# AdaLN block with rank-1-scaled attention and an MLP: new on-chip addresses for the TensorE operands, and the two products of one weight tile issued in pairs

## The reference

```python
mod = (_silu(L0_c) @ L0_wmod).reshape(8, 6, 1, -1)
sa, ca, ga, sb, cb, gb = (mod[:, i] for i in range(6))
ga = (2 * (ga >= 0) - 1) * jnp.maximum(jnp.abs(ga), 0.25)      # the same for gb
h = _layernorm(x) * (1 + ca) + sa
scores = jnp.einsum('nsd,ntd->nst', h * w_lhs, h * w_rhs)
x = x + ga * jnp.einsum('nst,ntd->nsd', softmax(scores, axis=2), h)
h = _layernorm(x) * (1 + cb) + sb
x = x + gb * (relu(h @ W1 + b1) @ W2 + b2)
```

## Time and profile before

| | us |
|---|---|
| median of 3 runs | 682.03 (681.68 to 682.57) |
| the profiled execution, whole | 681.68 |
| its span in the trace | 679.9 |
| TensorE matmul busy | 675.1 (99% of the span) |
| TensorE weight load busy | 624.6 (92%) |
| VectorE busy | 546.8 (80%) |
| ScalarE busy | 500.2 (74%) |
| GpSimd busy | 295.6 (43%) |

### The profile page before, as it was taken

How to read it: one execution, slowest core, us unless ns; L and a number is a source line. 1 busy time by engine, 2 the same in 40 slices (tenths; PEclk the granted TensorE clock), 3 DMA queues, 4 the chain that set the end, 5 groups by cost and what they waited for, 6 DMA issues and landing times.

```text
span 679.9 us, 13532 instructions
## 1 busy us (share of the span) xinstructions
PE 675.1 (99%) x4551; PEld 624.6 (92%) x4551; DVE 546.8 (80%) x1139; ACT 500.2 (74%) x749; POOL 295.6 (43%) x311
## 2 busy tenths in 40 slices
PE   9999999999999999999999999999999999999998
PEld 8688899998999999998999989999899999999997
DVE  4798889887998879988799887988799887778321
ACT  2377787976789777895888958888678976747562
POOL 3551365225353345442545235542535333615543
PEclk9999999999999999999999999999999999999999
DMA  8131664237632478025671266423662246212210
GB/s 295 56 79 66 196 181 148 72 108 235 193 86 87 121 225 246 38 86 160 192 204 62 93 195 200 129 62 126 217 199 75 83 138 208 89 35 71 85 40 31
DMA packets 72897, 88.57 MB, mean 130 GB/s; under 512 B 6880, under 2 KB 64800, under 8 KB 72864
## 3 DMA queue, kind: packets, MB, share of 16 engines
q1 hardware_dynamic: 72864, 88.15, 42.1%
HBM read 51.66 MB, written 36.47 MB: 130 GB/s over the span
## 4 chain that ended last, share of the span: by engine, by line
PE 99%; DVE 0%; DMA 0%; issue 0%; SPq 0%
PE col L666 9%; PE col L667 9%; PE col L668 9%; PE acc L588 8%; PE acc L589 8%; PE acc L594 8%; PE score L773 8%; PE score L768 8%; PE score L770 8%; PE score L656 4%; PE score L657 4%; PE score L655 4%; PE score L761 4%; PE score L629 2%; PE score L557 1%; PE score L733 1%
## 5 line engine op out<-in xcount | busy, mean ns | idle before, releaser
L1256 POOL TENSOR_TENSOR hid_lo<-hid,hid_hi 128x512 fp32r<-128x512 f32 x127 | 176.2, 1390 | 259.8 <-ACT hid_hi L798 259.3
L794 ACT ACTIVATE hid<-col,b1T 128x512 f32<-128x512 f32 x128 | 87.2, 682 | 73.9 <-PE col L668 72.0
L588 PE MATMUL acc<-W2hi,hid_hi 128*128 128x256 f32 x480 | 119.3, 282 | 0.0
L589 PE MATMUL acc<-W2lo,hid_hi 128*128 128x256 f32 x480 | 117.9, 279 | 0.0
L666 PE MATMUL col<-h2hi,W1hi 128*128 128x512 f32 x256 | 100.3, 392 | 0.0
L667 PE MATMUL col<-h2lo,W1hi 128*128 128x512 f32 x256 | 100.2, 391 | 0.0
L668 PE MATMUL col<-h2hi,W1lo 128*128 128x512 f32 x256 | 99.7, 389 | 0.0
L798 ACT ACTIVATE hid_hi<-hid 128x512 fp32r<-128x512 f32 x128 | 81.0, 633 | 23.9 <-PE acc L594 16.3
L588 PEld LDWEIGHTS acc<-W2hi,hid_hi 128*128 128x128 f32 x480 | 90.6, 189 | 1.4
L589 PEld LDWEIGHTS acc<-W2lo,hid_hi 128*128 128x128 f32 x480 | 90.6, 189 | 1.3
L594 PE MATMUL acc<-W2hi,hid_lo 128*128 128x256 f32 x480 | 77.7, 279 | 0.0
(11 more groups left out here) (168 smaller groups left out, 1476.9 us busy)
## 6 DMA issues: line engine op xcount, KB each, us to landing
block_rows<-blocks SPq DMA_DIRECT2D x29, 512.0 KB, 2.8
blocks<-block_rows SPq DMA_DIRECT2D x116, 128.0 KB, 2.9
x_cur<-x SPq DMA_DIRECT2D x16, 512.0 KB, 3.9
ln_t<-x SPq DMA_DIRECT2D x14, 512.0 KB, 5.2
score_blocks<-stages SPq DMA_DIRECT2D x14, 512.0 KB, 3.1
S<-score_blocks SPq DMA_DIRECT2D x56, 128.0 KB, 2.9
S<-quarter_blocks SPq DMA_DIRECT2D x56, 96.0 KB, 2.5
out<-x_mlp SPq DMA_DIRECT2D x8, 512.0 KB, 5.1
```

The lines of the kernel that those rows point to most:

```text
L588: nc.tensor.matmul(o, hi, W2hi[:, it, :], start=(it == 0 and (apart or t % 2 == 0)), stop=False, skip_group_check=True)
L589: nc.tensor.matmul(o, hi, W2lo[:, it, :], start=False, stop=False, skip_group_check=True)
L794: nc.scalar.activation(hid[:, n % 2, :], col[n % 2][:], ACT.Relu, bias=b1T[:, n % FT:n % FT + 1]).then_inc(col_read, 1)
L1256: G.tensor_tensor(hid_lo[:, n % RING, :], hid[:, n % 2, :], hid_hi[:, n % RING, :].bitcast(F32), ALU.subtract).then_inc(hid_lo_done, 1)
```

## The change

It has four parts.

1. Phi, Plo and the fp32 tensors that lie under them lose their padding: a row is 128 words. The staging tensors under Phi get their own names (`stage`, `stage_lr`).
2. Small tensors move. The seven that belong to the weights' roots and signs go ahead of `mod_cols`, the statistics and maxima to the very end, behind h2lo. `before_h2` goes, and `behind_V` (96 words) comes in behind V.
3. In V the low part moves to words 0 to 255 and the high part to words 260 to 515. What writes and reads them follows.
4. In AV.n the two products with the same Phi tile stand one behind the other (tile by tile), where before all 8 of the one came ahead of all 8 of the other.

No instruction is added or removed on any engine, and no wait. In the built program the starts are now, in bytes: W1hi 17024, W2hi 33408 (both as before), Phi 87328, Plo 99616, Lhi 111904, Rhi 128288, V 144672, hid_hi 198560, h2hi 210848.

While one matmul's moving operand is read, the weight tile of the next is loaded. The distance from the start of that moving operand to the start of that weight tile, modulo 128 bytes, is:

| lines before | distance before | distance after |
|---|---|---|
| SC (L655 to L657) | 0 | 0 |
| F (L666 to L668) | 0 | 96 |
| G (L588, L589, L594) | 64 | 32 |
| AV, low part with Phi (L768) | 80 | goes through 0, 96, 64, 32 with the tile |
| AV, high part with Phi (L770) | 96 | goes through 112, 80, 48, 16 |
| AV, high part with Plo (L773) | 96 | goes through 112, 80, 48, 16 |

Before, a Phi row is 544 bytes and a V row 2080 bytes, both 32 bytes over a multiple of 512, so the distance stays the same from tile to tile. After, a Phi row is 512 bytes. The starts themselves, modulo 64 bytes: before, 0 for all but every second tile of Phi, Plo and V (32) and the low part of V (16 or 48); after, 0 for W1 and W2, 32 for Phi, Plo, L, R, hid and h2, 32 and 0 in turns for V's low part, 48 and 16 in turns for its high part.

The diff:

```diff
--- before.py
+++ after.py
@@ -224,7 +224,6 @@
     VW = D + 2
 
     VP = D + 4
-    PW = P + 8
     assert T == 8 and DK == 2 and FT == 8 and HR == 512 and NB >= 4
     NF = 2 * FT
 
@@ -263,6 +262,9 @@
         b1T, b2T = sb("b1T", [P, FT]), sb("b2T", [P, DK])
         wl, wr = sb("wl", [P, DK]), sb("wr", [P, DK])
 
+        w_sign, w_abs, w_root = sb("w_sign", [P, 2, DK]), sb("w_abs", [P, 2, DK]), sb("w_root", [P, 2, DK])
+        root_power, root, root_r, sign_r = sb("root_power", [P, 2, DK]), sb("root", [P, DK]), sb("root_r", [P, DK]), sb("sign_r", [P, DK])
+
         mod_cols = sb("mod_cols", [P, NB, 4 * DK])
         mod_a, mod_b = sb("mod_a", [P, 2 * DK]), sb("mod_b", [P, 2 * DK])
 
@@ -282,32 +284,19 @@
 
 
 
-
-
-        with nc.sbuf_tensor("stages", [P, RING, T * PW], F32) as stages, nc.sbuf_tensor("soft_rows", [P, RING, T, PW], F32) as soft_rows:
-            stage = [stages[:, h, 0:T * P].rearrange("p (u v t r) -> p u v t r", u=Q, v=HT, t=2) for h in range(2)]
-            soft = soft_rows[:, :, :, 0:P]
-            stage_q = [soft_rows[:, RING - 1].rearrange("p a b -> p (a b)")[:, 0:Q * TURNS * QP], stages[:, RING - 1, 0:Q * TURNS * QP]]
-        Phi_rows, Plo_rows = sb("Phi", [P, RING, T, PW], F32R), sb("Plo", [P, RING, T, PW], F32R)
-        Phi, Plo = Phi_rows[:, :, :, 0:P], Plo_rows[:, :, :, 0:P]
+        with nc.sbuf_tensor("stage", [P, 2, Q, HT, 2, QP], F32) as stage, \
+                nc.sbuf_tensor("stage_lr", [P, T, P], F32) as stage_lr, nc.sbuf_tensor("soft", [P, RING, T, P], F32) as soft:
+            stage_q = [q.rearrange("p a b -> p (a b)")[:, 0:Q * TURNS * QP] for q in (soft[:, RING - 1], stage_lr[:])]
+        Phi, Plo = sb("Phi", [P, RING, T, P], F32R), sb("Plo", [P, RING, T, P], F32R)
         with nc.sbuf_tensor("L_first", [P, DK, ROWS], F32) as L_first, nc.sbuf_tensor("R_first", [P, DK, ROWS], F32) as R_first:
             pass
         Lhi, Llo = sb("Lhi", [P, DK, ROWS], F32R), sb("Llo", [P, DK, ROWS], F32R)
         Rhi, Rlo = sb("Rhi", [P, DK, ROWS], F32R), sb("Rlo", [P, DK, ROWS], F32R)
-        stats, stats1 = sb("stats", [P, HT, 6]), sb("stats1", [P, HT, 6])
-        mv1, nm1, rs1 = sb("mv1", [P, T, 2]), sb("nm1", [P, T]), sb("rs1", [P, T])
-        mv2, nm2, rs2 = sb("mv2", [P, T, 2]), sb("nm2", [P, T]), sb("rs2", [P, T])
         with nc.sbuf_tensor("V_unsplit", [P, T, 2 * VP], F32) as V_unsplit:
             V_first = V_unsplit[:, :, VP:VP + VW]
         V = sb("V", [P, T, 2 * VP], F32R)
 
-        var_eps, half_power = sb("var_eps", [P, HT]), sb("half_power", [P, HT])
-        row_max, part_max = sb("row_max", [P, T]), sb("part_max", [P, 2, 4, HT])
-        inv_sum = sb("inv_sum", [P, 1])
-        nb1, nb2 = sb("nb1", [P, T]), sb("nb2", [P, T])
-        mod_l, mod_r = sb("mod_l", [P, 2 * DK]), sb("mod_r", [P, 2 * DK])
-
-        root, sign_r = sb("root", [P, DK]), sb("sign_r", [P, DK])
+        sb("behind_V", [P, 96])
         x_cur = sb("x_cur", [P, T, D])
         x_mlp = sb("x_mlp", [P, T, D])
 
@@ -320,10 +309,15 @@
         featT = sb("featT", [P, DK, HR])
         hid = sb("hid", [P, 2, HR])
         hid_hi, hid_lo = sb("hid_hi", [P, RING, HR], F32R), sb("hid_lo", [P, RING, HR], F32R)
-        w_sign, w_abs, w_root = sb("w_sign", [P, 2, DK]), sb("w_abs", [P, 2, DK]), sb("w_root", [P, 2, DK])
-        root_power, root_r = sb("root_power", [P, 2, DK]), sb("root_r", [P, DK])
-        sb("before_h2", [P, 8])
         h2hi, h2lo = sb("h2hi", [P, DK, ROWS], F32R), sb("h2lo", [P, DK, ROWS], F32R)
+        stats, stats1 = sb("stats", [P, HT, 6]), sb("stats1", [P, HT, 6])
+        mv1, nm1, rs1 = sb("mv1", [P, T, 2]), sb("nm1", [P, T]), sb("rs1", [P, T])
+        mv2, nm2, rs2 = sb("mv2", [P, T, 2]), sb("nm2", [P, T]), sb("rs2", [P, T])
+        var_eps, half_power = sb("var_eps", [P, HT]), sb("half_power", [P, HT])
+        row_max, part_max = sb("row_max", [P, T]), sb("part_max", [P, 2, 4, HT])
+        inv_sum = sb("inv_sum", [P, 1])
+        nb1, nb2 = sb("nb1", [P, T]), sb("nb2", [P, T])
+        mod_l, mod_r = sb("mod_l", [P, 2 * DK]), sb("mod_r", [P, 2 * DK])
 
 
         wmod_a = S[:, 7, :].rearrange("p (k n) -> p k n", k=DK)
@@ -484,7 +478,7 @@
                     elif kind == "SW":
 
                         sp.wait_ge(stage_done, HT * (b - 1) + 2 * n + 2)
-                        sp.dma_start(score_blocks[n], stages[:, n, 0:T * P]).then_inc(stage_stored[n], 16)
+                        sp.dma_start(score_blocks[n], stage[:, n].rearrange("p u v t r -> p (u v t r)")).then_inc(stage_stored[n], 16)
                     elif kind == "SR":
 
                         sp.wait_ge(stage_stored[n], 16 * b)
@@ -765,12 +759,11 @@
                         if n == 0:
                             pe.wait_ge(v_done, 2 * b)
                         for t in range(T):
-                            nc.tensor.matmul(o, Phi[:, slot, t, :], V[:, t, VP:VP + VW], start=(t == 0), stop=False)
-                        for t in range(T):
-                            nc.tensor.matmul(o[:, 0:D], Phi[:, slot, t, :], V[:, t, 0:D], start=False, stop=False)
+                            nc.tensor.matmul(o, Phi[:, slot, t, :], V[:, t, 0:VW], start=(t == 0), stop=False)
+                            nc.tensor.matmul(o[:, 0:D], Phi[:, slot, t, :], V[:, t, VP:VP + D], start=False, stop=False)
                         pe.wait_ge(plo_done, T * (b - 1) + n + 1)
                         for t in range(T):
-                            last = nc.tensor.matmul(o, Plo[:, slot, t, :], V[:, t, 0:VW], start=False, stop=(t == T - 1))
+                            last = nc.tensor.matmul(o, Plo[:, slot, t, :], V[:, t, VP:VP + VW], start=False, stop=(t == T - 1))
                         last.then_inc(av_done, 1)
 
             over_batches(pe, part)
@@ -872,7 +865,7 @@
 
                         act.wait_ge(v_ln, HT * (2 * b + n - 1))
                         act.wait_ge(av_done, T * b)
-                        nc.scalar.activation(V[:, n * HT:(n + 1) * HT, 0:D], ln_v[:], ACT.Copy).then_inc(v_hi, 1)
+                        nc.scalar.activation(V[:, n * HT:(n + 1) * HT, VP:VP + D], ln_v[:], ACT.Copy).then_inc(v_hi, 1)
                     elif kind == "EX":
 
                         if ph is PH["first"]:
@@ -1037,7 +1030,7 @@
                             V_.tensor_tensor(tile[:, 0:HT], s_upper[:, :, t, :], most.broadcast_to([P, HT, P]), ALU.subtract).then_inc(sub_done, 1)
                     elif kind == "ST":
                         dve.wait_ge(scores_read, T * b + n + 1)
-                        V_.transpose(stage[n // 2][:, :, :, n % 2, :], s_flat[:, 7 * n * P:7 * n * P + HR].rearrange("p (v u r) -> p u v r", v=HT, r=QP)).then_inc(stage_done, 1)
+                        V_.transpose(stage[:, n // 2, :, :, n % 2, :], s_flat[:, 7 * n * P:7 * n * P + HR].rearrange("p (v u r) -> p u v r", v=HT, r=QP)).then_inc(stage_done, 1)
                     elif kind == "QT":
 
                         dve.wait_ge(scores_read, T * b + (n + 1) * HT)
@@ -1137,7 +1130,7 @@
 
                         tiles = slice(n * HT, (n + 1) * HT)
                         dve.wait_ge(v_hi, 2 * b + n - 1)
-                        V_.tensor_tensor(V[:, tiles, VP:VP + D], ln_v[:], V[:, tiles, 0:D].bitcast(F32), ALU.subtract).then_inc(v_done, 1)
+                        V_.tensor_tensor(V[:, tiles, 0:D], ln_v[:], V[:, tiles, VP:VP + D].bitcast(F32), ALU.subtract).then_inc(v_done, 1)
                     elif kind in ("BH", "B2"):
                         if kind == "BH":
                             turn = ph.turn(b, "TH", n)
```

## The result

| | before | after |
|---|---|---|
| median of 5 runs, us | 681.75 (681.46 to 682.57) | 686.39 (685.74 to 687.78) |
| ratio, 95% interval | | 1.0067 [1.0053, 1.0083] |
| span of the profiled execution, us | 679.9 | 685.1 |

The change costs 4.6 us. The forecast was 686.5.

What follows compares the result with a forecast made beforehand. TensorE's back-to-back matmuls were taken to bound the kernel; AV 0, G +3.3 and F +1.2 gave +4.5 us on 681.7, so 686.2, and 0.35 up to the median: 686.5 us, range 677.5 to 691.0.

Steps and rivals of the forecast that it cites:

- What bounds the kernel: TensorE is busy 675.1 of 679.9 us with one 1.5 us wait; time is the distances between starts of 4551 matmuls.
- Distance as the cause: In F, G and AV, time above 0.443 ns per column was taken to go with the distance between the two reads.
- The first rival: All fp32r matmuls keep their rhythm because distance is a mere companion of something else: 682.0 us, chance 0.22.
- A place where the distance isn't a multiple of 64: Matmuls of 256 columns there were priced at 118.3 ns, from AV's L770, against G's 113.3 to 117.5.
- G: +3.3: G's distance goes from 64 to 32, so its blocks take 1.42 us each: 3.3 us slower.
- seven quick blocks of batch 3: Of 16 G blocks counted in batch 3, seven took 1.36 to 1.38 us and nine 1.41; each quick one would gain 0.05.
- F: +1.2: F's distance goes from 0 to 96; half of the possible 2.4 us loss was taken, as reading is half shared.
- upper bound of 2.4: F's late form no longer dies out: ten blocks a batch rise by 0.03 us, +2.4 us in all.
- AV: 0: AV's new distances, which vary by tile, were taken to cost nothing; bounds -7.8 and +3.1 us.
- the faster rival: AV falls to G's late form, -2.6 us, with F and G unchanged: 679.4 us; at the quick rate 674.2; chance 0.28.
- The pairs: 0: Putting AV's two products with one Phi tile together gains nothing, since each matmul still loads its own weights.
- SC, the other engines, the waits: 0: SC's distance stays 0, PE waits for neither VectorE nor ScalarE, and no DMA moves: no effect.

Runs made afterwards that it cites:

- hid_plus32: Kernel before with hid_hi and hid_lo alone moved by 32 bytes, so only G's distance changes (64 to 96): 684.33 us, 1.0031.
- h2_plus32: Kernel before with h2hi and h2lo alone moved by 32 bytes, so only F's distance changes (0 to 224 modulo 256): 683.42 us, 1.0020.
- f_g_only: Kernel before with only F's and G's distances as in the change (224 and 32 modulo 256), AV and its layout as before: 688.21 us, 1.0097.
- all_plus32: Kernel before with every TensorE operand but ident starting 32 bytes later, all distances between them kept: 681.60 us, 0.9996.
- probe_distance: Kernel before with blocks of 16 equal matmuls appended at its end, varying width, moving start and distance; 256 columns: 113.3 ns at distance 64, 117.4 to 120.3 at others.
- v_aligned: Changed kernel with G's and F's distances at 64 and 128 modulo 256, V's rows widened to 544 words and Plo and V moved: 686.36 us, 1.0062.
- probe_period: Kernel before with other equal matmuls appended, widths 256 to 512, distances up to 1216 bytes; 512 columns: 3.65 us per sixteen at 256 bytes, 3.73 at 384.
- after_unpaired: Changed kernel with AV's first 16 matmuls back in the old order, all low part and then all high part: 686.93 us, 1.0071.
- after_realigned: Changed kernel with G's distance back at 64 and F's at 0 modulo 128 (128 modulo 256), the first repair: 683.24 us, 1.0016.
- after_realigned2: Changed kernel with G's distance at 64 and F's at 0 modulo 256, as in the kernel before: 683.16 us, 1.0017.

## Why the prediction was right, and where its terms were not

**What bounds the kernel.** Right. One wait, PE at 99%, full granted clock, and the difference of the medians (4.64 us) is near the difference of the block sums (4.2). The missing 0.4 us is less than the 1.0 us by which the start-up differs from execution to execution.

**Distance as the cause.** It was put forward as a correlation. hid_plus32, h2_plus32 and f_g_only make it a cause, all_plus32 excludes the starts (for 32 bytes). The first rival, that nothing moves, is refuted, and with it what it drew from a page: the Trainium skill, in "TensorE: Matmul & The Clock Gate", Part 2, step 1, has loading the next tile's weights take no read bandwidth from the running matmul. The page doesn't speak of addresses, the rival read from it that they are worth nothing. In probe_distance a matmul of 256 columns with a new weight tile costs 113.3 or up to 120.3 ns by the address of that tile alone, and moving both reads by 32 bytes together changes nothing (all_plus32). At least in this form of matmul the timing of the two reads isn't free of each other.

**Its form was wrong.** "A place where the distance isn't a multiple of 64" was too coarse in three ways. The period is 256 and not 128: the table in "The change" gave F 96 where it is 224, and the first repair put F at 128 and called it 0. In rows of equal matmuls the quick distances depend on the width: 64 and 192 for 256 columns, 0, 16 and 240 for 512, none for 258. And AV's lateness doesn't come from its 80 and 96 alone: two thirds of it are 258 wide, which no distance made quick in such rows, and v_aligned, which put the 256-wide line on 64 and 192, got nothing. That the 258-wide matmuls are what holds AV late is argued from this, not shown: no run gave AV another width.

**G: +3.3, measured +2.9.** Right in mechanism and size. All 126 blocks are at 1.41 us or more, as was to be seen if it was right. The prediction's seven quick blocks of batch 3 are six at or under 1.38 us and G.10 at 1.46, which like G.4 stands behind transposes. G.10 rose with the six, by 0.05 us.

**F: +1.2, measured +3.1.** Mis-sized, and above its upper bound of 2.4. The half that I took had no row behind it. The reason given, that only half of such a matmul's reading is shared with a weight load, is shown by no run: F's weight loads are 0.19 us long in the trace, and its matmuls start 0.23 us apart. The late form no longer dies out in any of the 128 blocks, and it is also later than the old one, 1.391 to 1.403 us in batch 3 where the late ones were at 1.387. The bound was wrong because it took the late form of distance 0 as the late form of any distance. probe_period has 233.3 ns at 224, F's distance after the change, against 226.7 at the end of its row at 0, which is 1.40 us for a block of six.

**AV: 0, measured -1.6.** Mis-sized, inside its bounds. The 258-wide line with Phi went from 120.6 to 117.8 ns per matmul, the 256-wide from 118.3 to 118.7, the one with Plo from 120.9 to 119.7. The gain is largest at the second, third and fourth tile, with distances of 224, 192 and 160 modulo 256: there the 258-wide matmul with Phi takes 116.1, 115.7 and 116.6 ns on average where it took 120.7, 122.8 and 119.0. The distances alone don't bring it, for in after_unpaired, which has the same ones in the old order, these three take 121.4, 120.7 and 120.3. So why AV is quicker stays open beyond the split into 0.9 us without the pairs and 0.7 with them. The direction was the faster rival's, but not its size (-2.6), and not its condition, that F and G don't care about 32 bytes.

**The pairs: 0.** Nearly right for AV on the old addresses (-0.1), not on the new ones (-0.7), and in neither case was there a term for what AV's order does to G (+1.0 on the old addresses).

**SC, the other engines, the waits: 0.** Right, SC -0.2 us, PE's waits unchanged.

So the sum of +4.5 met +4.6 with F's error of +1.9 and AV's of -1.6 cancelling each other. The sign and G's part were earned, the last digit was luck. One thing was missing from the whole sum: it gave each kind of block its own term, and the runs show that a block's time also depends on the blocks ahead of it (G -2.2 us in h2_plus32, whose G isn't touched). In the change this didn't show in G, as no quick G block was left to gain or lose (179.9 us there, 179.8 in f_g_only).

**What stays open.** Why these distances are the quick ones, and what exactly one block hands to the next. The runs show that the history counts (G -2.2 behind a changed F, G +1.0 behind a changed AV), but none isolates what is handed on. It is one reason why three forecasts that added up terms block by block missed by 2.5 to 7 us (after_realigned also had the period wrong). No arrangement tried here is faster than the kernel before. all_plus32 equals it and nothing lies below.

## What to carry to other kernels

Where TensorE is busy 99% of the time and its starts in the timeline have two rhythms for one kind of matmul, the addresses of the operands are a parameter of the kernel: moving two operands by 8 words each cost 1.0% here (f_g_only), and giving the change two of its distances back won 0.5% of its 0.7% (after_realigned2). None of these moves made the kernel before faster. Measure it in the kernel itself and not only by a probe, since a block's rhythm also depends on the block ahead. And when any tensor ahead of an operand changes its size, write down the distances (start of weight tile less start of moving operand, modulo 256 bytes) before and after, or the gain of the edit may be paid back elsewhere, as AV's 1.6 us were.

## What the runs showed of the hardware

- In fp32r with a new weight tile for each matmul, the distance modulo 256 bytes between moving operand and next weight tile moves the time of a matmul from 113.3 to 120.3 ns (256 columns) and from 226.6 to 234.4 ns (512 columns). Starts alone, moved by 32 bytes together, do nothing (0.9996), while with the moving operand 16 bytes on, another distance is the quick one at 512 columns (96 instead of 0 and 16), and the slowest takes 236.5 ns.
- 113.3, 173.2 and 226.6 ns for 256, 384 and 512 columns are the lowest in rows of equal matmuls. The first and the last are 0.443 ns per column, the middle one 0.451. With 258 columns such a row never came below 116.9 ns. In AV, where they stand in turns with 256-wide ones, single tiles are at 115.7 on average (after).
- At one and the same distance modulo 256 two stable forms exist (113.3 and 117.8 ns at 64 and 192 with 256 columns in probe_period). In the kernel the blocks ahead decide between them: the same G block at the same addresses takes 1.413 us in before and 1.367 in h2_plus32.
